# One core, four layers: scale and shift as rows, earlier edge work, reordered starts, and row loads ahead of weight loads in the expert layer

## The reference

```
x = L0(x, A_grid, B_grid, dt)   # max(f + dt*(-grad(A f) + 0.5*grad2(B f)), 0), one-sided at the borders
# L1: adaptive layer norm, attention with a bias and a mask, feed-forward
emb = silu(sin_emb(timestep)) @ W_ada + b_ada; scale, shift = split(emb)
x = ln(x) * (1 + scale) + shift
probs = softmax(where(mask, -inf, q @ k.T / sqrt(32) + attention_bias))   # 16 heads
x = x + probs @ v @ Wo + bo
x = x + gelu2((ln(x)*g2 + beta2) @ W1 + b1) @ W2 + b2                     # 512 -> 2048 -> 512
# L2: one expert for each batch, gathered by index
h = gelu(x @ Wi[e] + bi[e]) @ Wo[e] + bo[e]; y = ln(h + x) * gamma[e] + beta[e]
# L3: y + strength * (y @ basis @ basis.T[:, :32] @ resp_w.T + biases),
#     basis = gram_schmidt(U) @ gram_schmidt(V).T; strength from mean over rows, a gate and a score
```

## Time and profile before

| | us |
|---|---|
| median of 3 runs | 3105.91 (3099.93 to 3112.11) |
| profiled execution, its time | 3107.88 |
| its span, first to last instruction | 3106.0 |
| TensorE busy | 2800.0 (90%) |
| VectorE busy | 1902.1 (61%) |
| ScalarE busy | 1121.9 (36%) |
| GpSimd busy | 1043.1 (34%) |

### The profile page before, as it was taken

One profiled execution on the slowest core, in us unless ns is written; L12 is line 12 of the kernel. 1 busy time (PEld: TensorE's weight loads), 2 busy tenths in 40 slices (PEclk: granted clock), 3 DMA queues, 4 the chain that ended last, 5 costly groups with the idle time before them and its releaser, 6 DMA issues. The chain is left out here.

```text
span 3106.0 us, 45892 instructions
## 1 busy us (share of the span) xinstructions
PE 2800.0 (90%) x14065; PEld 2263.7 (73%) x14065; DVE 1902.1 (61%) x3722; ACT 1121.9 (36%) x2256; POOL 1043.1 (34%) x751
## 2 busy tenths in 40 slices
PE   6964999999999999969999999999699889988986
PEld 3423788888888888857777877778577777767775
DVE  8954778777787878765444344442565564665543
ACT  1114777677776778641111111111111111211111
POOL 1005576566656767453001110010332222222210
PEclk9986999999999999989999999999899999999998
DMA  4224776767676676642100000000442333233311
GB/s 163 97 87 145 201 200 184 207 180 200 189 203 191 184 206 187 182 124 82 35 28 28 1 28 28 28 14 1 133 150 95 110 108 113 85 112 102 99 48 34
DMA packets 255730, 356.47 MB, mean 115 GB/s; under 512 B 26570, under 2 KB 113738, under 8 KB 252794
## 3 DMA queue, kind: packets, MB, share of 16 engines
q1 hardware_dynamic: 253754, 350.26, 37.8%
q0 software_dynamic: 1728, 3.13, 0.4%
HBM read 268.91 MB, written 34.05 MB: 98 GB/s over the span
## 5 line engine op out<-in xcount | busy, mean ns | idle before, releaser
L819 POOL TENSOR_TENSOR at_bias<-at_bias,at_mask 128x1024 f32<-128x1024 f32 x224 | 480.8, 2149 | 370.5 <-DMA at_bias<-in_fside_Bx16xSxS 369.1
L1218 DVE TENSOR_TENSOR at_pL<-at_bank_probT,at_pH 128x512 fp32r<-128x512 f32 x512 | 351.4, 686 | 212.1 <-ACT at_pH L930 210.4
L923 ACT ACTIVATE at_y<-at_bias,at_nmax 128x512 f32<-128x512 f32 x512 | 368.4, 720 | 57.9 <-DVE at_nmax L1212 56.6
L930 ACT ACTIVATE at_pH<-at_bank_probT 128x512 fp32r<-128x512 f32 x512 | 304.3, 594 | 207.8 <-PE at_bank_probT L1073 202.7
L1212 DVE CUSTOM_DVE_ANT_0 at_bias<-at_bias,at_bank_score 128x512 f32<-128x512 f32 x512 | 346.5, 677 | 2.9 <-ACT at_y L923 1.1
L1589 POOL TENSOR_SCALAR expert_WH<-expert_stage 128x1024 fp32r<-128x1024 f32 x128 | 165.3, 1291 | 538.1 <-PE expert_bank_out L98 369.3
L1073 PE MATMUL at_bank_probT<-at_ident,at_y 128*128 128x128 f32 x2048 | 312.3, 275 | 35.0 <-DVE at_pL L1218 29.1
L1921 DVE CAST ff_gH<-ff_g 128x512 fp32r<-128x512 f32 x128 | 68.0, 532 | 426.3 <-ACT ff_g L1662 426.2
L1662 ACT ACTIVATE ff_g<-ff_bank_hid,ff_b1c 128x512 f32<-128x512 f32 x128 | 88.2, 689 | 646.8 <-PE ff_bank_hid L98 646.8
L1073 PEld LDWEIGHTS at_bank_probT<-at_ident,at_y 128*128 128x128 f32 x2048 | 246.9, 141 | 95.4 <-ACT at_y L923 28.0
L1662 ACT ACTIVATE expert_g<-expert_bank_hid,expert_b1c 128x512 f32<-128x512 f32 x128 | 88.2, 689 | 622.1 <-PE expert_bank_hid L98 616.9
(11 more groups left out here) (309 smaller groups left out, 6337.8 us busy)
## 6 DMA issues: line engine op xcount, KB each, us to landing
at_bias<-in_fside_Bx16xSxS SPq DMA_DIRECT2D x256, 512.0 KB, 4.6
expert_stage<-in_L_cond_Wi SPq DMA_DIRECT2D x128, 256.0 KB, 2.7
expert_stage<-in_L_cond_Wo SPq DMA_DIRECT2D x128, 256.0 KB, 2.8
at_q<-at_nat SPq DMA_DIRECT2D x384, 64.0 KB, 3.5
at_k<-at_nat SPq DMA_DIRECT2D x384, 64.0 KB, 2.9
st_f<-in_x SPq DMA_DIRECT2D x8, 1024.0 KB, 7.3
x_after_layer<-st_y SPq DMA_DIRECT2D x8, 1024.0 KB, 4.8
at_x<-x_after_layer SPq DMA_DIRECT2D x32, 256.0 KB, 4.0
```

Of the source, the lines that this page charges most:

```text
L819: pool.tensor_tensor(bias[i % NB][:, :, :], bias[i % NB][:, :, :], mask[:, 2 * i % R:2 * i % R + 2, :], ALU.add).then_inc(s_bm, 1)
L923: act.activation(prob[u % 2][:, :], bias[u // 2 % NB][:, u % 2, :], ACT.Exp, scale=-1.0, bias=nmax[:, u % 4:u % 4 + 1], accum_out=sums[:, ...
L930: act.activation(pH[u // 2 % 2][:, :, u % 2, :], pT[u % 2][:, :].rearrange("p (k q) -> p k q", q=P), ACT.Copy).then_inc(s_pth, 1)
L1218: dve.tensor_tensor(pL[u // 2 % 2][:, :, u % 2, :], pT[u % 2][:, :].rearrange("p (k q) -> p k q", q=P), f32(pH[u // 2 % 2][:, :, u % 2, :] ...
```

## The change

In `stencil` the products of W_ada are turned round: `emb` is stationary and W_ada moves, so that scale and shift come out as rows, and SP stores them to DRAM there. The edge rows are loaded and their first 12 steps made before `final` of the last batch; only the rows of `border_pre` are loaded after it.

```diff
-        bada = sb("bada", [P, 2 * C])
+        bada = sb("bada", [B, 2, D])
+        ada = sb("ada", [B, 2, D])
...
+                if n == 1:
+                    sp.wait_ge(s_a, 26)
+                    sp.dma_start(ada_rows, ada[:, :, :]).then_inc(s_ada, 16)
...
+            for slot in range(2):
+                sp.wait_ge(s_edge[slot], 96 * (B // 2))
+            for rows, src in sides:
+                sp.dma_start(eo[rows, :, :, :].rearrange("b o r c -> b (o r) c"), src[:, 0:12, :]).then_inc(s_el, 16)
             border_pre(B - 1)
             for slot in range(2):
-                sp.wait_ge(s_edge[slot], 96 * (B // 2))
                 sp.wait_ge(s_row[slot], 32 * (B // 2))
...
+            for rows, src in sides:
+                sp.dma_start(ep[rows, :], src[:, 12, :]).then_inc(s_ep, 16)
             store(B - 1)
...
-            for m in range(2 * C):
+            for m in range(2):
                 for c in range(C):
-                    t_ = pe.matmul(pa[:, m * B:(m + 1) * B], w_ada[c // 2][:, c % 2, m * P:(m + 1) * P], emb[:, c, :],
+                    t_ = pe.matmul(pa[:, m, :], emb[:, c, :], w_ada[c // 2][:, c % 2, m * D:(m + 1) * D],
...
-            final(B - 1)
-
-            dve.wait_ge(s_el, 64)
-            dve.wait_ge(s_edt, 16 * 2 * QS)
+
+            dve.wait_ge(s_el, 32)
...
+            final(B - 1)
             dve.wait_ge(s_ed, 12)
+            dve.wait_ge(s_ep, 32)
```

```diff
             for r in range(R):
                 load_x(0, 0, r)
+            load_scale_shift(0)
             for k, name in enumerate(("Wq", "Wk", "Wv", "Wo")):
...
-                if k == 0:
-                    sp.wait_ge(s_adac, 1)
-                    sp.dma_start(ada_rows.rearrange("m b p -> (m b) p"), adat).then_inc(s_adad, 16)
                 if k == 1:
                     load_mask(0)
-                    sp.wait_ge(s_adad, 16)
-                    load_scale_shift(0)
-                    for i in range(3):
-                        load_bias(0, i)
+                if k == 2:
+                    load_bias(0, 0)
+                if k == 3:
+                    load_bias(0, 1)
+                    load_bias(0, 2)
...
-            for k in range(2 * R):
-                scale_shift(0, 0, k)
...
             weights_high(0)
             weights_high(1)
-            weights_high(2)
+            for m in range(C):
+                x_high(0, m)
             act.wait_ge(s_const, 64)
             act.wait_ge(s_bq, 1)
-            for m in range(C):
-                x_high(0, m)
             q_high(0, 0)
             k_high(0, 0)
+            weights_high(2)
             copy_vT(0, 0)
             v_high(0, 0)
+            exp(0, 0)
             weights_high(3)
-            exp(0, 0)
```

In the feed-forward, `gram_schmidt` on TensorE runs at f % 4 == 1 in place of 0, and between `hidden` and `output`:

```diff
                 for f in range(FC):
                     hidden(n, f)
+                    if not expert:
+                        gram_schmidt(n, f)
                     if f > 0:
                         output(n, f - 1)
...
-                    if not expert:
-                        gram_schmidt(n, f)
```

In the expert layer the rows of the next batch are loaded ahead of the weight unit of the same step, the last batch's transposes use four banks and no longer wait for one another's copies, and ACT computes one throwaway exponential ahead of the gate's:

```diff
+        def y_bank(n, m):
+            return (pt[0], pg[0], pg[1], po[0])[m] if alone(n) else pt[0]
...
-                    load_unit(e, n + 1, f)
                     if f >= 14 and not first:
                         for r in ((0, 1) if f == 14 else (2, 3)):
                             load_row(n + 1, 1 - slot, j if slot == 0 else j + 1, r)
+                    load_unit(e, n + 1, f)
...
+                if f == 10 and alone(n):
+                    act.activation(warm[:, :], gw[:, 2:3], ACT.Exp, scale=-1.0)
...
-                    else:
+                    elif not alone(n):
                         pe.wait_ge(s_yl, n * C + m)
                         pe.wait_ge(s_yh, n * C + m)
```

More of the change, by code:

```diff
@@ L503, in stencil, with attention @@
     names.clear()
-def attention(nc, a, x_in, x_out, ada, ada_rows):
+def attention(nc, a, x_in, x_out, ada_rows):
     with ExitStack() as ctx:
@@ L1248, in _ @@
             mean_var(0)
+            dve.wait_ge(s_ab, 32)
+            for r in range(R):
+                dve.wait_ge(s_xhat, r + 1)
+                dve.tensor_tensor(x[0][:, r, :], x[0][:, r, :], scale[:, :], ALU.mult).then_inc(s_first, 1)
+            for r in range(R):
+                dve.wait_ge(s_first, r + 1)
+                dve.tensor_tensor(x[0][:, r, :], x[0][:, r, :], shift[:, :], ALU.add).then_inc(s_ln, 2)
             weights_low(0)
+            dve.wait_ge(s_const, 64)
+            dve.tensor_scalar(bc[:, 0, :], bc[:, 0, :], 1.0 / math.sqrt(HD), None, ALU.mult).then_inc(s_bq, 1)
             weights_low(1)
-            weights_low(2)
             dve.wait_ge(s_bq, 1)
@@ L2125, in build @@
     edges = nc.dram_tensor("border_rows", (2, 4, B, 13, D // 4), F32).ap()
[L2126 removed]
+    ada_rows = nc.dram_tensor("scale_shift_rows", (B, 2, D), F32).ap()
     with ExitStack() as ctx:
[L2128 to L2130 removed]
+        stencil(nc, a, x0, edges, ada_rows)
+        attention(nc, a, x0, x1, ada_rows)
         uv = ctx.enter_context(nc.sbuf_tensor("uv", [P, 2 * C, RANK], F32))
```

64 lines of the change are left out of this document (27 added, 37 removed).

## The result

| | us |
|---|---|
| before, median of 4 runs | 3108.18 (3099.93 to 3112.11) |
| changed kernel, median of 4 runs | 3019.11 (3016.24 to 3019.54) |
| ratio | 0.9715, 95% interval 0.9693 to 0.9737: 2.9% faster |
| span of the profiled execution | 3106.0 before, 3017.2 after: 88.8 less |

The forecast was 3019.4 and a gain of 86.5 us; measured are 88.8 (spans) to 89.1 us (medians). The total came out, but not its parts, and that is what the rest is about.

What follows compares the result with a forecast made beforehand. The prediction took TensorE, its idle time and low clock, to bound the kernel. Its terms summed to 86.5 us, taking the profiled 3107.9 to 3021.4 and, with the median 1.97 lower, 3019.4; range 3010 to 3030, chance 0.55.

Steps and rivals of the forecast that it cites:

- Step 1: Stencil: W_ada's products with 512 columns take 9.1 us, batch 0 starts at 35.5 at full clock; gain 6.3 us.
- the low bound: Stencil: only 2.2 us gained if the narrow stationary side keeps the clock low through W_ada's products.
- Step 2: End of the stencil: edge steps made during DVE's wait, last stores then wait for the store of x; gain 2.9 us.
- Step 3: Start of attention: first projection earlier by 16.7 us, part given back at v's projection with low clock; net 13.8 us.
- Step 4: Feed-forward: `hidden` of step 1 fills the 2.55 us wait for `prod` in eight batches; gain 20 us.
- Step 5: Expert layer: rows ahead of units cut the wait to 1.1 us, clock stays high; 6.5 us a boundary, 39 in all.
- Rival B: Expert layer: rows win only what the DMA queue loses; gain 12 to 21 us, time 3039; chance 0.18.
- Step 6: Tail: transposes run on without waiting for low copies, gain 4.7 us; throwaway exponential hides nothing, adds 0.2; net 4.5.
- C: Start of attention gives back most, through late weights, slowed DVE and low clock; net 5 us, time 3028; chance 0.12.
- E: Attention: its tiles move in memory and slow the score steps; at 0.25 us each, time 3147; chance 0.02.
- F: Nothing moves: the waits only change their names, such as another 6 us at each expert-layer boundary; chance 0.03.
- D: Expert layer gains wait and clock in full, 7.8 us a boundary, and W_ada's products 6.7; time 3010; chance 0.10.

Runs made afterwards that it cites:

- att_order: Changed kernel with x_high and x_low ahead of the second weight's halves, and Wv split ahead of q and k, at attention's start: 3015.5 us, ratio 0.9711.
- all_together: Changed kernel with the edits of att_order, unit_behind and warm_early plus six unread matmuls ahead of the expert layer's waits for rows: 3001.3 us, ratio 0.9659.
- ff_filler: Kernel before with nine unread matmuls put ahead of the wait for `prod` at the start of each feed-forward batch: 3093.5 us, ratio 0.9968.
- unit_behind: Changed kernel with unit 14 fetched behind all four rows of x in the expert layer: 3010.2 us, ratio 0.9695.
- last_layers: Stencil and attention of the kernel before, with feed-forward, expert layer and tail of the changed kernel: 3037.3 us, ratio 0.9785.
- warm_early: Changed kernel with the throwaway exponential moved from behind the copies of `feats` to step 0 of the last tail: 3018.7 us (one execution).
- rows_only: Kernel before with only the rows of x fetched ahead of units 14 and 15 in the expert layer: 3078.3 us, ratio 0.9906.

## Why the prediction was right, and where it was not

*What bounds the kernel* held: what could be placed lies in waits of TensorE or in its clock, and no other engine became the bound. Not placed are small pieces of attention and the two gaps of TensorE.

*Step 1*, products of W_ada, right in size, partly for another reason. The rows:

```profile
26.07 3.58 PE L338 MATMUL st_bank_sum<-st_V,st_emb 128*8 128x512 f32 x4 [26.07 <-DMA st_Qp<-in_L_cond_W_ada]
...
33.69 1.88 PE L338 MATMUL st_bank_sum<-st_Qp,st_emb 128*8 128x512 f32 x4
35.50 1.13 PE L353 MATMUL st_bank_sum<-st_V,st_mats 128*128 128x512 f32 x2
```

9.4 us where 9.1 were predicted, batch 0 at 35.5 as predicted and at full clock (1.13 for two records, 2.06 in the earlier trace rows). The clock did rise under the narrow stationary side, between the first four records (3.58 us) and the third four, some 5 us after the first matmul; the low bound falls away. The last sum of the stencil came 6.6 us earlier (predicted 6.3).

*Step 2*, right: 9.9 - 6.6 = 3.2 us against 2.9. The store of x went out at 207.33 and the last stores at 211.34, 4.0 us later.

*Step 3*, right in its chain, 3.7 us too small in the whole of attention. The first projection stands 27.6 us after the first load of x (predicted 25.8 to 27, before 43.0), v's another 13.0 later (13.4), with the low clock that was expected. Of the 15.4 us at the first projection 12.0 are left at v's. What came on top, up to 17.5 at the end of the phase, lies behind the first chunk in small pieces: a shorter wait for the first row maxima, and waits for the stacked k of 5.8 us in all and not 9.0. Over all kernels attention takes 1143.4 to 1153.0 with the old start and 1128.5 to 1132.9 with the new one (without att_order and all_together, which change it again). These pieces were not traced one by one.

*Step 4*, the wait right, the clock missed. ff_filler leaves 20 us for the wait, as said. What failed is the reading of the earlier trace rows, which the prediction gives in step 3 and by which step 4 put the clock at nothing: "A gap of 2.55 us leaves the clock high (the eight small matmuls behind it take 1.10 us)". The clock falls in five of seven batches, and in four of these only 0.9 to 1.9 us after the wait. The term lacked some 10 us. The prediction's sentence that the Trainium skill's page "TensorE: Matmul & The Clock Gate", section "HAM oscillation — how this bites in real kernels", would have the clock stay high over a short wait, "as rows 7 show", falls with that reading. The section's own case is a kernel whose clock falls in each wait of about 3 to 5 us for data; here it fell behind waits of 2.5 us too.

*Step 5*, the direction right, the size wrong: 4.1 us a boundary and not 6.5. Three parts failed. The landing: "the load goes out at 2519.1, lands at 2523.1" used the time of a load that had only a unit beside it; among stores, four rows and a unit it took about 1.5 us more at the boundary shown (1.0 by the medians of the loads), and the wait was 2.9 us and not 1.1. unit_behind shows 1 us of it to be the unit. The store: at three of the six boundaries it goes out 0.4 to 1.0 us later against TensorE than in the earlier trace rows (7.2 us ahead of its end there), which the prediction had left as it was; last_layers ties this to the new first two phases. (The prediction's own sum has a slip of 0.3 us: 2515.3 + 3.3 is 2518.6, not 2518.9.) The clock: with waits of 2.2 to 3.6 us it still falls in five of six batches, so that instead of 1.8 us some 0.7 were won (24.7 us less the 20.4 of waits, over six). Rival B named the mechanism, and stood too low in the gain (12 to 21); the truth lay between B and the forecast.

*Step 6*, the waits right, the clock on top: 5.5 from the banks (4.7 predicted) and 1.5 by the moment of the clock. That the throwaway exponential hides nothing where it stands was right; warm_early shows 1 us for it elsewhere.

*Rivals*: C did not come, E and F had no ground; D's clock was real, but in the feed-forward.

## What to carry to other kernels

A wait of TensorE costs its length and then, often, a stretch at half clock that can begin up to 2 us after the wait is over; look at the first 5 us behind it and count over several repetitions, never in one row. Where a wait of 2 to 3 us can't be removed, matmuls that nobody reads, put in front of it, can take the clock's part away (10 to 13 us in eight batches here). And price a moved transfer by what travels with it at its new place, not by its latency at the old one, and check that the transfer it waits for still goes out when it did: here an earlier phase moved that by up to 1 us.

## What the runs showed of the hardware

- Behind the same wait of 2.5 us the clock fell in some batches and not in others, in one execution: 0.98, 0.98 and 1.00 in the windows above. In rows_only it fell behind waits of 2.0 and 1.5 us and not behind one of 2.55. A wait of 6.2 us at a boundary cost 1.5 us of clock, one of 3.3 about 1.0, not in proportion. The Trainium skill's page "TensorE: Matmul & The Clock Gate", section "What's actually happening", says that the number of slow matmuls at a start varies from run to run; the tails agree, with 6.2 and 7.7 us for the same instructions.
- The clock can rise while TensorE does nothing but transposes: in the tail of the changed kernel it rose 2.6 us after the first of them (1.11 us for four, then 0.60 for four). In other kernels the same last four still took 1.05.
- At a boundary a row's load took 3.6 to 3.9 us (medians) from issue to landing with a unit beside it, and 4.1 to 5.7, by kernel and boundary, among two stores, four rows and a unit.
- One and the same DMA issue of SP took 0.37 us or 0.8 to 1.4, the long value at every second boundary and only with the new first two phases, which had ended some 1000 us earlier; the stores behind it left later by about as much. Why is open.
